# State space scan: each step as two interleaved chains of two heads in place of one chain of four

## The reference, cut to what matters

```python
zt = Ac[None, None] * (0.5 * dt)[..., None]
den = 1.0 - zt
abar = (1.0 + zt) / den
u_in = Bc * ((dt * x_sum)[..., None] / den)

def step(h, inp):
    a, b = inp
    h = a * h + b
    return (h, h)
_, hs = jax.lax.scan(step, h0, (jnp.swapaxes(abar, 0, 1), jnp.swapaxes(u_in, 0, 1)))
y_red = jnp.real(Cc * hs).sum(axis=-1)
```

## Time and profile before

| | |
|---|---|
| time, median of 3 runs | 1044.02 us (1042.91 to 1050.02) |
| the profiled execution | 1050.32 us, of which its span is 1048.5 us |
| busy in the span: PE, PEld, DVE | 855.5, 520.2, 746.7 us |
| busy in the span: ACT, POOL | 561.9, 204.5 us |
| the recurrence, first to last operation | 299.8 to 546.0 us from the span's start |

### The profile page before, as it was taken

One profiled execution on the slowest core, in us unless ns is written; L12 is line 12 of the kernel. 1 busy time (PEld: TensorE's weight loads), 2 busy tenths in 40 slices (PEclk: granted clock), 3 DMA queues, 4 the chain that ended last, 5 costly groups with the idle time before them and its releaser, 6 DMA issues. The chain is left out here.

```text
span 1048.5 us, 26783 instructions
## 1 busy us (share of the span) xinstructions
PE 855.5 (82%) x9567; PEld 520.2 (50%) x9567; DVE 746.7 (71%) x2473; ACT 561.9 (54%) x1398; POOL 204.5 (20%) x217
## 2 busy tenths in 40 slices
PE   5899999995865896888633696887969999999686
PEld 2577777773322342332211574654646666666443
DVE  5588888883589999899996793555654565665557
ACT  3698888885856666584131674443333323223234
POOL 1466666662000000000000120003200000000136
PEclk9899999998977898898776797996999999999779
DMA  7111111100000000000004404002720000000001
GB/s 235 32 43 42 40 40 40 40 1 1 1 0 1 1 1 0 1 1 0 1 0 103 67 1 163 4 4 98 278 108 1 2 0 0 0 0 1 1 11 30
DMA packets 23157, 36.54 MB, mean 35 GB/s; under 512 B 5668, under 2 KB 19748, under 8 KB 20644
## 3 DMA queue, kind: packets, MB, share of 16 engines
q1 hardware_dynamic: 23080, 35.53, 11.2%
HBM read 34.48 MB, written 1.05 MB: 34 GB/s over the span
## 5 line engine op out<-in xcount | busy, mean ns | idle before, releaser
L381 ACT ACTIVATE xa_prob<-xa_s,xa_nmax 128x257 f32<-128x257 f32 x256 | 128.1, 503 | 22.7 <-DVE xa_nmax L466 21.0
L568 POOL TENSOR_TENSOR xa_prob<-xa_prob,xa_rinv 128x1028 f32<-128x1028 f32 x64 | 121.5, 1900 | 77.8 <-DVE xa_rinv L473 76.6
L466 DVE CUSTOM_DVE_ANT_0 xa_s<-xa_s_ps,xa_nbias 128x257 f32<-128x257 f32 x256 | 93.2, 421 | 12.2 <-ACT xa_prob L381 6.4
L1489 POOL TENSOR_TENSOR mo_disp_t<-mo_disp_t,mo_rst 128x256 f32<-128x256 f32 x16 | 9.8, 616 | 378.0 <-DVE mo_rst L1469 378.0
L2197 ACT COPY ca_z<-ca_z_ps 128x512 f32<-128x512 f32 x64 | 37.5, 585 | 84.6 <-PE ca_z_ps L2114 84.6
L2114 PEld LDWEIGHTS ca_z_ps<-ca_xn_t,ca_m_t 128*128 128x128 f32 x512 | 62.0, 198 | 26.8 <-issue 24.3
L242 PE MATMUL xa_t_ps<-identity,xa_prob 128*128 128x128 f32 x512 | 69.4, 279 | 4.2 <-ACT xa_p_t L390 2.1
L456 DVE COPY xa_kvs<-xa_kv_ps 128x512 f32<-128x512 f32 x64 | 44.1, 690 | 36.6 <-PE xa_kv_ps L216 36.6
L2114 PE MATMUL ca_z_ps<-ca_xn_t,ca_m_t 128*128 128x128 f32 x512 | 67.9, 288 | 1.3 <-ACT ca_xn_t L2191 1.3
L242 PEld LDWEIGHTS xa_t_ps<-identity,xa_prob 128*128 128x128 f32 x512 | 54.7, 141 | 25.9 <-issue 25.9
L390 ACT COPY xa_p_t<-xa_t_ps 128x1024 f32<-128x1024 f32 x64 | 63.4, 991 | 3.1 <-PE xa_t_ps L242 3.1
(11 more groups left out here) (327 smaller groups left out, 1989.3 us busy)
## 6 DMA issues: line engine op xcount, KB each, us to landing
xa_ctx_t<-in_ctx_t SPq DMA_DIRECT2D x64, 128.5 KB, 2.1
room<-in_ctx_t SPq DMA_DIRECT2D x8, 1028.0 KB, 6.8
room<-in_ctx_n SPq DMA_DIRECT2D x8, 1024.0 KB, 4.8
ss_wx<-in_ss_wx SPq DMA_DIRECT2D x1, 2048.0 KB, 7.9
xres<-in_x SPq DMA_DIRECT2D x4, 256.0 KB, 5.1
out_x<-xres SPq DMA_DIRECT2D x4, 256.0 KB, 2.3
ma_mask_u<-in_mask SPq DMA_DIRECT2D x4, 128.5 KB
room<-in_ca_wk SPq DMA_DIRECT2D x1, 512.0 KB, 5.2
```

What stands on the lines that cost most here:

```text
L381: nc.scalar.activation(prob[:, r, g, :], s_sb[:, b, g, :], ACT.Exp, bias=nmax[:, r, g:g + 1], scale=-1.0, accum_out=rsum[:, r, g:g + 1]).t ...
L466: nc.vector.tensor_tensor_reduce(out=s_sb[:, b, g, :], in0=s_ps[:, g, 0:S], in1=nbias[:, g, :], scale=1.0, scalar=3e38, op0=ALU.add, op1=A ...
L568: nc.gpsimd.tensor_tensor(prob[:, r, :, :], prob[:, r, :, :], bc(rinv[:, r, :].rearrange("p (g o) -> p g o", o=1), (P, G, S)), ALU.mult).t ...
```

## The change

Each step is done as two chains, one for heads 0 and 1 (q = 0) and one for heads 2 and 3 (q = 1). Every operation of the step is issued twice with half of the elements (2 x 2 x 16 = 64), once for each chain, one right behind the other. `step_done` becomes two semaphores, one for each chain, so that an operation waits for its own chain alone. A step issues ten operations of 64 elements in place of five of 128. The two operations of 1060 and 1061 stay together within a chain. The gaps of `fill` stay behind the first, the middle and the last of them: gap 0 behind both additions to `g`, gap 1 behind all four products (before: behind the addition of t1), gap 2 behind both additions of t2. Step 0 has its call of gap 0 too now, in which the schedule has nothing.

```diff
+        step_done = sem("step_done_low"), sem("step_done_high")
...
-                n, now, j = done_before(c, l), slice(CB * l, CB * l + CB), c % 2
-                wl, ar = w[:, j, :, :, now], bc(a_r[:, j, :, now].unsqueeze(1), (P, 2, H, CB))
+                n, now, last, j = done_before(c, l), slice(CB * l, CB * l + CB), slice(CB * l - CB, CB * l), c % 2
+                heads = (slice(0, 2), slice(2, 4))
                 if l == 0:
...
-                    if c >= 1:
-                        dve.wait_ge(step_done, n)
-                    src = wl
+                    src = [w[:, j, :, hs, now] for hs in heads]
                 else:
-                    dve.wait_ge(step_done, n)
-                    nc.vector.tensor_tensor(g[:, :, :, :], w[:, j, :, :, CB * l - CB:CB * l], wl, ALU.add).then_inc(step_done, 1)
+                    src = [g[:, :, hs, :] for hs in heads]
+                    for q, hs in enumerate(heads):
+                        dve.wait_ge(step_done[q], n)
+                        nc.vector.tensor_tensor(src[q], w[:, j, :, hs, last], w[:, j, :, hs, now], ALU.add).then_inc(step_done[q], 1)
                     n += 1
-                    fill(c, l, 0)
-                    dve.wait_ge(step_done, n)
-                    src = g[:, :, :, :]
-                nc.vector.tensor_tensor(t1[:, :, :, :], ar, src, ALU.mult).then_inc(step_done, 1)
-                nc.vector.tensor_tensor(t2[:, :, :, :], a_i[:, j, :, :, now], src[:, ::-1], ALU.mult).then_inc(step_done, 1)
-                dve.wait_ge(step_done, n + (2 if l == 0 else 1))
-                nc.vector.tensor_tensor(wl, wl, t1[:, :, :, :], ALU.add).then_inc(step_done, 1)
+                fill(c, l, 0)
+                for q, hs in enumerate(heads):
+                    if n > 0:
+                        dve.wait_ge(step_done[q], n)
+                    nc.vector.tensor_tensor(t1[:, :, hs, :], bc(a_r[:, j, hs, now].unsqueeze(1), (P, 2, 2, CB)), src[q], ALU.mult).then_inc(step_done[q], 1)
+                    nc.vector.tensor_tensor(t2[:, :, hs, :], a_i[:, j, :, hs, now], src[q][:, ::-1], ALU.mult).then_inc(step_done[q], 1)
                 fill(c, l, 1)
-                dve.wait_ge(step_done, n + 3)
-                nc.vector.tensor_tensor(wl, wl, t2[:, :, :, :], ALU.add).then_inc(step_done, 1)
+                for q, hs in enumerate(heads):
+                    dve.wait_ge(step_done[q], n + (2 if l == 0 else 1))
+                    nc.vector.tensor_tensor(w[:, j, :, hs, now], w[:, j, :, hs, now], t1[:, :, hs, :], ALU.add).then_inc(step_done[q], 1)
+                for q, hs in enumerate(heads):
+                    dve.wait_ge(step_done[q], n + 3)
+                    nc.vector.tensor_tensor(w[:, j, :, hs, now], w[:, j, :, hs, now], t2[:, :, hs, :], ALU.add).then_inc(step_done[q], 1)
                 fill(c, l, 2)

             def outputs(c, h):
                 if h == 0:
-                    dve.wait_ge(step_done, done_before(c + 1, 0))
+                    for q in range(2):
+                        dve.wait_ge(step_done[q], done_before(c + 1, 0))
```

More of the change, by code:

```diff
@@ L671, in state_space @@
          a_i_ready, a_n_ready, b_mm, bsq_ready, b_ready, ssb_mm, rb_ready, sb_ready, sbs_mm, w_ready,
-         step_done, c_mm, csq_ready, c_ready, ssc_mm, rc_ready, prod_ready, y_mm, yr_ready, ysp_mm, ys_ready,
+         c_mm, csq_ready, c_ready, ssc_mm, rc_ready, prod_ready, y_mm, yr_ready, ysp_mm, ys_ready,
          o_mm, res_ready, stats_ready, dve_past) = (sem(n) for n in (
@@ L676, in state_space @@
             "a_i_ready", "a_n_ready", "b_mm", "bsq_ready", "b_ready", "ssb_mm", "rb_ready", "sb_ready", "sbs_mm", "w_ready",
-            "step_done", "c_mm", "csq_ready", "c_ready", "ssc_mm", "rc_ready", "prod_ready", "y_mm", "yr_ready", "ysp_mm", "ys_ready",
+            "c_mm", "csq_ready", "c_ready", "ssc_mm", "rc_ready", "prod_ready", "y_mm", "yr_ready", "ysp_mm", "ys_ready",
             "o_mm", "res_ready", "stats_ready", "dve_past"))
+        step_done = sem("step_done_low"), sem("step_done_high")
         norm = NormScales(k, "ss", mv, rstd, nmr)
```

## The result

The changed kernel takes 1056.07 us (median of 6 runs, 1050.16 to 1057.11), the kernel before beside it 1047.51 us (6 runs, 1042.91 to 1050.22). The ratio is 1.0081, with a 95% interval from 1.0052 to 1.011: slower by 8.5 us. The profiled execution of the changed kernel took 1052.2 us.

What follows compares the result with a forecast made beforehand. VectorE, busy 94% of the recurrence, was taken as the bound. Own operations +10.3 us, less 1.2 us hidden, gave +9.1 us on the median of 1044.0: 1053 us, range 1046 to 1070.

Steps and rivals of the forecast that it cites:

- The price of a 64-element operation: In the recurrence, VectorE was to take 0.134 us for each 64-element operation; 1272 of them make 171.0 us.
- the 160.7 counted before: VectorE's own recurrence operations before the change, with their stalls: 160.7 us, set against 171.0 after, difference +10.3 us.
- the rival of a costlier short operation: In the recurrence, short operations cost more or their results come later: 1073 or 1071 us; chance 0.18.
- the faster case: In the recurrence, the fixed part of 0.067 us shrinks with the operation; at 0.115 us an operation, 1030 us; chance 0.03.
- No stall is left: In the recurrence, VectorE never waits for itself: starts 0.13 to 0.14 us apart, a step without fillers 1.34 us.
- Every operation waits for the end of the one before: Rival in the recurrence: interleaving buys nothing, an operation takes 0.22 us, +118 us, 1162 us; chance 0.02.
- The fixed part: Size-independent cost of each VectorE operation, taken as 0.067 us from the rows and paid ten times a step, not five.
- what is hidden: Of VectorE's 5.6 us of waits for TensorE in the recurrence, only 1.2 us were to hide added work.
- round trips: Four of six VectorE waits in the recurrence run VectorE, TensorE, VectorE; their length was not to change.
- The rival in which most is hidden: In the recurrence, all 5.6 us of waits shrink to nothing: +4.7 us, 1049 us; chance 0.15.
- Outside the recurrence nothing changes.: For the rest of the kernel, no change was forecast; another stretch moving would make the prediction wrong.

Runs made afterwards that it cites:

- one semaphore: Changed kernel's operations in its order, with one semaphore for both chains instead of two; 1057.84 us, ratio 1.0104 to the kernel before.
- four chains: Kernel before with each step as four chains of one head, twenty operations of 32 elements a step; 1144.45 us, ratio 1.0924.
- the split in steps without fillers: Kernel before with two chains only in the 56 steps without any filler, line 1061 whole there; ratio 0.9992.
- nine operations: Changed kernel with line 1061 kept as one 128-element operation in all steps; 1050.65 us, ratio 1.0041 to the kernel before.
- the best forms: Kernel before with each step operation split or whole, and gap 1 placed, as counted cheapest, 955 operations; 1044.58 us, ratio 0.9992.
- unused operations in empty gaps: Kernel before with an unused 64-element operation in each of the 259 gaps without a filler; ratio 1.0038.

## Why the prediction was right, point by point

It said 1053.0 us, +9.1 or 0.9%; the runs gave +8.5 us, from 5.4 to 11.5. The direction and the size held, by a sum whose terms did not all hold; that the whole came out so close is in part luck.

- **The price of a 64-element operation**, the term on which all hung: 0.134 predicted, 0.1354 us measured, with a duration of 0.22 us as said. 1272 x 0.1354 = 172.2 us, against the 160.7 counted before: +11.5 and not +10.3. But the 160.7 was too low as well: by its rows the kernel before spends 161.4 us on its own operations, and the recurrence less the waits grew by 10.8 us. The straight line holds down to 32 elements. With only 1.2 us hidden, as the prediction had it, 0.1354 us would have made +10.3 us, all but the 10.4 us from which it called the kernel slower. So the rival of a costlier short operation is out, and so is the faster case, in which the fixed part shrinks with the operation.
- **No stall is left**: held. Starts are even, a step without fillers is 1.36 us (1.34 predicted), a filled one 2.81 us (2.80). The gain is small where there was something to cover, the loss is large where a filler already stood.
- **Every operation waits for the end of the one before** (1162 us): out. Starts are 0.135 us apart at a duration of 0.22. The Trainium skill has the rule in "VectorE: DVE Perf Modes", section "The DRAIN you can't avoid", but not without exception, as the prediction has it: the same paragraph says that a next operation that is not held starts earlier. The trace agrees with the exception.
- **The count of operations** does not decide by itself. The Trainium skill advises to keep it low, in "VectorE: DVE Perf Modes", section "Rules for kernel authors". The trace agrees in part: among the kernels split throughout fewer operations are faster (2544, 1272 and 1144 take 337.7, 251.6 and 247.2 us), but 955 operations take 239.9 us and the 636 of the kernel before 245.9. An operation more pays where it removes a stall.
- **The fixed part** is 68 ns here, from three sizes, and the slope 1.04 ns an element. The Trainium skill gives about 75 ns and 1.0417 ns, in "Vector Engine (DVE) Microarchitecture Reference", section "Measured stream behaviour on trn2". The trace agrees with the slope, and for the fixed part the measured 68 ns decides.
- **The step that failed: what is hidden.** "The others are round trips (VectorE, TensorE, VectorE) whose length does not change. I take 1.2 us off": it was 5.1 of the 5.6 us. The two waits of `gated_y`, 2.1 us in the earlier trace rows, stand behind 3.7 us of other matmuls in TensorE's own order; up to 0.8 us of what went is TensorE's higher clock in chunk 2. What was left are the two short round trips ahead of `scaled_inputs` (`input_scale`, `spread_scales`, `scaled_inputs`): 0.17 us each before and 0.27 after. The rival in which most is hidden named 4.7 us net, at 0.15; its mechanism came nearest to what the recurrence did (+5.7). Chunk 2, where 3.1 us of waits stood, grew by 0.9 us and not by 3.8.
- **The second that failed: "Outside the recurrence nothing changes."** The tail grew by 1.8 us.
- The errors are +0.5 us of work (10.8 in place of 10.3; +1.2 after, less +0.7 before), -3.9 us of hiding and +1.8 us of tail. Together they come to -1.6 us: 10.8 - 5.1 + 1.8 = 7.5 us, which is what the two profiles of the layer show, against 9.1 forecast. The medians' 8.5 us are no closer than their interval. The forecast is better than its parts: with the full 5.1 us taken off and no tail it would have been +5.2 us, just below the interval.

The tail can be read from two rows of TensorE at its end. Before:

```profile
550.83 3.67 PE L789 MATMUL ss_bank<-ss_w,ss_ones 128*32 128x512 f32 x16 [17.54 <-DVE ss_w L1073]
555.31 1.98 PE L797 MATMUL ss_bank<-ss_yr,ss_own_head 128*128 128x512 f32 x4 [0.82 <-DVE ss_yr L1082]
```

After:

```profile
556.85 3.67 PE L790 MATMUL ss_bank<-ss_w,ss_ones 128*32 128x512 f32 x16 [18.24 <-DVE ss_w L1078]
561.33 3.78 PE L798 MATMUL ss_bank<-ss_yr,ss_own_head 128*128 128x512 f32 x4 [0.82 <-DVE ss_yr L1087]
```

`reduce_y` is the same. `spread_y` takes 1.98 us before and 3.78 after: 1.80 us, the whole difference. The granted clock within `spread_y` is 1.00 before and 0.50 after, the two levels of 2.4 and 1.2 GHz; over the whole tail it is 0.72 against 0.62. The repeats gave the same durations: 1.98 us in the kernel before again, 3.78 in the changed kernel again. So it is stable from run to run. It does not come with the split as such: the tail is 18.1 to 18.4 us in the changed kernel, its repeat, one semaphore, four chains and the split in steps without fillers, and 15.9 to 16.4 in the kernel before, nine operations, the best forms and the rest. Nor does the length of TensorE's rest ahead of `reduce_y` decide it: rests of 14.26, 17.54 and 18.22 us (best forms, kernel before, unused operations in empty gaps) stand in front of the 1.98 us row, rests of 13.70, 18.24 and 32.22 us (split in steps without fillers, changed kernel, four chains) in front of the 3.78 us row. With the unused operations the clock came back even within `reduce_y`, which took 3.22 us in place of 3.67. What decides when the clock comes back is left open; 1.8 us of this result hang on it.

## What to carry to other kernels

A second chain pays only where an engine really waits for itself. Count each gap of the chain: an empty one holds a stall (0.123 us here), a filled one nothing, and each further operation costs its fixed part (0.068 us) in both. Split no operation whose result is needed late, and mind the stall at the seam between a split and a whole one. Before adding a wait of the bottleneck engine to the sum as fixed, look at the rows of the engine it waits for: if that engine is late by its own order, the wait can swallow what the change costs (here nearly half of it), and moving the hand-over a step later gave back 2.8 us of the recurrence without the change. Look at that engine's granted clock as well, here and behind the stretch that is changed.

## What the runs showed of the hardware that was not expected

- VectorE takes short operations (products and sums of two f32 tiles) at 0.068 us + 1.04 ns an element for each, down to 32 elements, with a semaphore wait and an increment on every one: 0.102, 0.135 and 0.201 us for 32, 64 and 128.
- A 64-element operation fits into the stall between two dependent 128-element operations for 0.012 us, so that stall is an idle issue slot and not a busy engine.
- The same four matmuls of 512 columns took 1.98 us in one kernel's tail and 3.78 in another's, repeatedly, and rests of nearly the same length (18.22 and 18.24 us) stood ahead of both; why, is not settled.
- The same matmuls of TensorE ahead of `reduce_y` in chunk 2 took 7.8 us at a granted clock of 0.58 and 7.0 at 0.76, each in both executions of its kernel: a change on VectorE alone moved TensorE's clock.
